# A fused test-time-training layer and mixture of experts: the low half of X1 taken ahead of the inverse's blocks, and the blocks spread by two rounded products

## The reference

```python
K, V, Q = x @ theta_K.T, x @ theta_V.T, x @ theta_Q.T
def step(W, b, k, v, q):
    g = 2 / 512 * (W @ k + b - v)
    W, b = W - 0.01 * outer(g, k), b - 0.01 * g
    return W, b, W @ q + b
x = layernorm(x + run_over_tokens(step))
shared = silu(x @ sW1 + sb1) @ sW2 + sb2
act = sqrt(softplus(x @ routing_W.T + expert_bias))
w, idx = top_k(act, 2)
x = layernorm(x + shared + sum_j w[j] * expert[idx[j]](x))
```

## Time and profile before

| | us |
|---|---|
| median of 3 runs (2300.41 to 2303.6) | 2301.88 |
| the profiled execution | 2296.03 |
| its span, first to last instruction | 2294.2 |
| PE busy | 2193.5 |
| DVE busy | 1548.6 |
| ACT busy | 891.7 |
| POOL busy | 1225.2 |
| mean granted clock of PE, 1 is full | 0.987 |

### The profile page before, as it was taken

One profiled execution on the slowest core, in us unless ns is written; L12 is line 12 of the kernel. 1 busy time (PEld: TensorE's weight loads), 2 busy tenths in 40 slices (PEclk: granted clock), 3 DMA queues, 4 the chain that ended last, 5 costly groups with the idle time before them and its releaser, 6 DMA issues.

```text
span 2294.2 us, 40089 instructions
## 1 busy us (share of the span) xinstructions
PE 2193.5 (96%) x12834; PEld 1899.8 (83%) x12834; DVE 1548.6 (68%) x3666; ACT 891.7 (39%) x1943; POOL 1225.2 (53%) x1168
## 2 busy tenths in 40 slices
PE   7999999999999999999999999999889999999896
PEld 6888888888888888888888888888779998998775
DVE  5666666666566778666656667775546545898798
ACT  4333333333333333333333334232255555555444
POOL 1344444433444333755544554346457777777777
PEclk9999999999999999999999999999989999999998
DMA  4211212122211111112211111110564435997996
GB/s 172 74 65 65 74 65 83 65 76 82 74 65 65 40 45 37 55 65 78 80 46 38 37 47 38 39 37 20 223 232 139 145 114 188 305 305 247 314 330 216
DMA packets 112201, 257.18 MB, mean 112 GB/s; under 512 B 21618, under 2 KB 23282, under 8 KB 109056
## 3 DMA queue, kind: packets, MB, share of 16 engines
q1 hardware_dynamic: 83776, 187.35, 23.5%
q0 software_dynamic: 27936, 67.22, 8.8%
q10 hardware_dynamic: 288, 0.04, 0.0%
HBM read 160.36 MB, written 105.26 MB: 116 GB/s over the span
## 4 chain that ended last, share of the span: by engine, by line
PE 77%; DVE 13%; issue 4%; POOL 2%; DMA 2%; ACT 1%; DVEq 0%; SPq 0%; POOLq 0%; ACTq 0%
PE banks L115 23%; PE banks L116 22%; PE banks L117 22%; PE banks L121 4%; DVE xc L1118 3%; PE banks L762 2%; PE banks L503 1%; PE banks L789 1%; DVE W L1115 1%; DVE b_Y L1118 1%; DVE banks L1115 1%; PE banks L541 1%; DVE X1l L1115 1%; DVE b_small L1661 1%; DMA W<-wd 1%
## 5 line engine op out<-in xcount | busy, mean ns | idle before, releaser
L115 PE MATMUL banks<-W 128*128 128x512 f32 (+1 forms) x2040 | 752.5, 369 | 10.8 <-DVE W L1115 7.6
L117 PE MATMUL banks<-W 128*128 128x512 f32 (+1 forms) x2040 | 718.0, 352 | 0.0
L116 PE MATMUL banks<-W 128*128 128x512 f32 (+1 forms) x2040 | 716.9, 351 | 0.0
L115 PEld LDWEIGHTS banks<-W 128*128 128x128 f32 x2040 | 387.9, 190 | 59.8 <-DVE W L1115 7.6
L117 PEld LDWEIGHTS banks<-W 128*128 128x128 f32 x2040 | 386.8, 190 | 54.8
L116 PEld LDWEIGHTS banks<-W 128*128 128x128 f32 x2040 | 388.3, 190 | 46.9
L1718 POOL TENSOR_TENSOR W<-S,W 128x512 fp32r<-128x512 f32 (+1 forms) x249 | 326.3, 1337 | 134.8 <-ACT W L833 134.2
L833 ACT ACTIVATE W<-banks 128x512 fp32r<-128x512 f32 x320 | 191.0, 598 | 503.3 <-DVE banks L1115 232.7
L1718 POOL TENSOR_TENSOR X<-X,B 128x1024 f32<-128x1024 f32 x32 | 76.8, 2401 | 459.0 <-DMA X<-in_x 459.0
L833 ACT ACTIVATE W<-S 128x512 fp32r<-128x512 f32 (+1 forms) x256 | 161.7, 653 | 219.5 <-DVE S L1115 213.2
L1115 DVE TENSOR_TENSOR W<-banks,W 128x512 fp32r<-128x512 f32 x192 | 132.4, 690 | 139.3 <-ACT W L833 139.2
(11 more groups left out here) (164 smaller groups left out, 4414.2 us busy)
## 6 DMA issues: line engine op xcount, KB each, us to landing
RG<-ys SPq DMA_DIRECT2D x128, 256.0 KB, 4.0
XT<-in_xT SPq DMA_DIRECT2D x32, 512.0 KB, 3.6
X<-in_x SPq DMA_DIRECT2D x32, 512.0 KB, 3.5
x1d<-X SPq DMA_DIRECT2D x64, 256.0 KB, 2.1
wd<-RG SPq DMA_DIRECT2D x32, 512.0 KB, 3.9
W<-wd SPq DMA_DIRECT2D x16, 1024.0 KB, 12.6
out<-b_Y SPq DMA_DIRECT2D x64, 256.0 KB, 4.4
zd<-X SPq DMA_DIRECT2D x52, 256.0 KB, 2.0
```

The lines of the kernel that those rows point to most:

```text
L115: e.matmul(o, ll, rh, start=start, stop=False, skip_group_check=True)
L116: e.matmul(o, lh, rl, start=False, stop=False, skip_group_check=True)
L117: return e.matmul(o, lh, rh, start=False, stop=stop, skip_group_check=True)
```

## The change

There are three edits.

1. In DVE's loop `turn_x1(t - 1, 1)`, which makes X1l of sequence 1, moves from behind `inv_m(t)` and the low half of P to a place ahead of `inv_m(t)`.
2. The compact form gd is written over the scores in their PSUM bank, where nothing else needs those columns once all three `rows_of` have read them; so these three now stand ahead of the sum. The unit products read it from there.
3. The compact form is split: gdh is its rounded part (scaled by -LRC), `rest` what is left of it, in PSUM too. The unit pattern multiplies each of them, four instructions instead of two, into two tiles in fp32r. `spread_blocks` is two products in fp32r with the block mask as the stationary operand, which is now an fp32r tile `blocks` of its own, made by a copy on ACT at the start. The two tiles take the memory of the inverse's halves (MTs, before MTh and MTl) and of the shared expert's hidden halves (Hp, before HH and HL), and waits keep the users apart: DVE's unit products wait for the last U and the last `down_x1`, ACT's `inv_end` and the writes of the hidden halves wait for the spread.

```diff
@@ memory
-        k.R = k.MM[:, 0:BLK]
-        k.xc, k.gd, k.rw = sb("xc", [NB, BS]), sb("gd", [NB, BS]), sb("rw", [KC, E])
+        k.Rp = k.MTs[:, 0:BLK], k.Hp[:, 0:BLK]
+        k.gdh = sb("gdh", [NB, BS], F32R)
+        k.xc, k.rw = sb("xc", [NB, BS]), sb("rw", [KC, E])
@@ tensor_program, spread_blocks
-        w.wait_ge(k.s_R, 2 * t + 2)
-        mm(e, o[:, 0:BLK], k.cst[:, 2, :], k.R).then_inc(k.s_Lb, 1)
+        w.wait_ge(k.s_R, 4 * t + 4)
+        mm(e, o[:, 0:BLK], k.blocks[:], k.Rp[1], True, False)
+        mm(e, o[:, 0:BLK], k.blocks[:], k.Rp[0], False, True).then_inc(k.s_Lb, 1)
@@ scalar_program
     def inv_end(t):
...
+        w.wait_ge(k.s_Lb, t + 1)
...
     def half_x1(t, b):
...
+        w.wait_ge(k.s_Lb, t + 2)
...
-    copy(k.onesr[:], k.RG[:, 0:P]).then_inc(k.s_ones, 1)
+    copy(k.onesr[:], k.RG[:, 0:P])
+    copy(k.blocks[:], k.RG[:, 2 * P:3 * P]).then_inc(k.s_ones, 1)
@@ vector_program, scores
-        rows_of(0).then_inc(k.s_sc, 1)
-        gd = k.gd[:]
-        w.wait_ge(k.s_sc, 4 * t + 2)
+        for n in range(NL):
+            z = rows_of(n)
+        z.then_inc(k.s_sc, 1)
+        gd = g[:, :, 0:BS]
+        w.wait_ge(k.s_sc, 6 * t + 2)
         e.tensor_reduce(gd, k.T1[:].rearrange("p b (k j) -> p b j k", k=NBL), AX.X, ALU.add).then_inc(k.s_sc, 1)
-        w.wait_ge(k.s_sc, 4 * t + 3)
-        w.wait_ge(k.s_MThi, t)
-        w.wait_ge(k.s_MTlo, t)
-        for h, o in enumerate(block_rows(k.R)):
-            rows = [P, HS, NB, (BS, HS)[h]]
-            own = unit_lr[:, h * HS:(h + 1) * HS].unsqueeze(2).unsqueeze(3)
-            tt(o, gd[:, :, h * HS:BS].unsqueeze(1).to_broadcast(rows), own.to_broadcast(rows), ALU.mult).then_inc(k.s_R, 1)
-        rows_of(1)
-        rows_of(2)
-        w.wait_ge(k.s_R, 2 * t + 2)
+        w.wait_ge(k.s_sc, 6 * t + 3)
+        e.tensor_scalar(k.gdh[:], gd, -LRC, None, ALU.mult).then_inc(k.s_sc, 1)
+        w.wait_ge(k.s_sc, 6 * t + 4)
+        rest = g[:, :, BS:2 * BS]
+        stt(rest, gd, -LRC, f32(k.gdh[:]), ALU.mult, ALU.subtract).then_inc(k.s_sc, 1)
+        w.wait_ge(k.s_sc, 6 * t + 5)
+        w.wait_ge(k.s_U, 2 * t)
+        w.wait_ge(k.s_dn1, min(2 * (t - 1), k.late))
+        for part, x, u in zip(k.Rp, (gd, rest), (unit_lr, unit)):
+            for h, o in enumerate(block_rows(part)):
+                rows = [P, HS, NB, (BS, HS)[h]]
+                own = u[:, h * HS:(h + 1) * HS].unsqueeze(2).unsqueeze(3)
+                tt(o, x[:, :, h * HS:BS].unsqueeze(1).to_broadcast(rows), own.to_broadcast(rows), ALU.mult).then_inc(k.s_R, 1)
+        w.wait_ge(k.s_R, 4 * t + 4)
@@ vector_program, the loop over t
+        if t > 0:
+            turn_x1(t - 1, 1)
         inv_m(t)
         next(first, None)
         if t > 0:
-            turn_x1(t - 1, 1)
             logits(t - 1, 0)
```

More of the change, by code:

```diff
@@ L30 @@
 NL = len(LEVELS)
-NCST = 3
 GROUPS = [14, 12, 6]
@@ L303, in first_memory @@
         k.X1p = sb("X1h", [KC, P], F32R), sb("X1l", [KC, P], F32R)
-        k.HF1, k.Hp1 = sb("HF1", [H]), (sb("HH1", [H], F32R), sb("HL1", [H], F32R))
+        k.HF1, k.Hp = sb("HF1", [H]), sb("Hp1", [2 * H], F32R)
+        k.Hp1 = k.Hp[:, 0:H], k.Hp[:, H:2 * H]
         k.brows, small = sb("brows", [D]), sb("small1", [40])
@@ L319, in first_memory @@
         k.ATp = sb("ATh", [NB, P], F32R), sb("ATl", [NB, P], F32R)
-        k.MTp = sb("MTh", [NB, P], F32R), sb("MTl", [NB, P], F32R)
-        k.onesr, k.cst = sb("onesr", [P], F32R), sb("cst", [NCST, P])
-        k.R = k.MM[:, 0:BLK]
-        k.xc, k.gd, k.rw = sb("xc", [NB, BS]), sb("gd", [NB, BS]), sb("rw", [KC, E])
+        k.MTs = sb("MTs", [2 * NB * P], F32R)
+        k.MTp = tuple(k.MTs[:, j * NB * P:(j + 1) * NB * P].rearrange("p (b n) -> p b n", b=NB) for j in range(2))
+        k.onesr, k.blocks, k.cst = sb("onesr", [P], F32R), sb("blocks", [P], F32R), sb("cst", [NB, P])
+        k.Rp = k.MTs[:, 0:BLK], k.Hp[:, 0:BLK]
+        k.gdh = sb("gdh", [NB, BS], F32R)
+        k.xc, k.rw = sb("xc", [NB, BS]), sb("rw", [KC, E])
 def second_memory(k):
@@ L545, in inv_t @@
         o = bank(w, ("T", t, n), k.s_T1, NL * t + n + 1)
-        w.wait_ge(k.s_sc, 4 * t + (4 if n else 2))
+        w.wait_ge(k.s_sc, 6 * t + 2)
         w.wait_ge(k.s_M0, NL * t + n + 1)
@@ L866, in scores @@
         kq = at["A", t].rearrange("p (b k n) -> p b k n", b=NB, k=2)[:, :, 1, :]
-        w.wait_ge(k.s_sc, 4 * t + 4)
+        w.wait_ge(k.s_sc, 6 * t + 6)
         w.wait_ge(k.s_O, 2 * t)
@@ L925, in half_x1 @@
         w.wait_ge(k.s_HS1, i + 1)
-        copy(k.Hp1[0][:], at["HB", t, b][:, 0:H]).then_inc(k.s_HH1, 1)
+        w.wait_ge(k.s_Lb, t + 2)
+        copy(k.Hp1[0], at["HB", t, b][:, 0:H]).then_inc(k.s_HH1, 1)
     def split_shared():
@@ L1100, in vector_program @@
     at = k.banks.at
-    mAT, mBD = k.cst[:, 0:2, :], k.cst[:, 2, :]
+    mAT, mBD = k.cst[:], f32(k.blocks[:])
     unit, unit_lr = k.smallc[:, 16:32], k.smallc[:, 136:152]
@@ L1141, in scores @@
         w.wait_ge(k.d_tab, 80)
+        w.wait_ge(k.s_ones, 1)
         w.wait_ge(k.s_T, NL * t)
@@ L1150, in scores @@
         stt(k.T1[:], g, 1.0, mBD.unsqueeze(1).to_broadcast(bc), ALU.add, ALU.mult).then_inc(k.s_sc, 1)
-        rows_of(0).then_inc(k.s_sc, 1)
-        gd = k.gd[:]
-        w.wait_ge(k.s_sc, 4 * t + 2)
-        e.tensor_reduce(gd, k.T1[:].rearrange("p b (k j) -> p b j k", k=NBL), AX.X, ALU.add).then_inc(k.s_sc, 1)
-        w.wait_ge(k.s_sc, 4 * t + 3)
-        w.wait_ge(k.s_MThi, t)
-        w.wait_ge(k.s_MTlo, t)
-        for h, o in enumerate(block_rows(k.R)):
-            rows = [P, HS, NB, (BS, HS)[h]]
-            own = unit_lr[:, h * HS:(h + 1) * HS].unsqueeze(2).unsqueeze(3)
-            tt(o, gd[:, :, h * HS:BS].unsqueeze(1).to_broadcast(rows), own.to_broadcast(rows), ALU.mult).then_inc(k.s_R, 1)
-        rows_of(1)
-        rows_of(2)
-        w.wait_ge(k.s_R, 2 * t + 2)
+        for n in range(NL):
+            z = rows_of(n)
+        z.then_inc(k.s_sc, 1)
+        gd = g[:, :, 0:BS]
+        w.wait_ge(k.s_sc, 6 * t + 2)
+        e.tensor_reduce(gd, k.T1[:].rearrange("p b (k j) -> p b j k", k=NBL), AX.X, ALU.add).then_inc(k.s_sc, 1)
+        w.wait_ge(k.s_sc, 6 * t + 3)
[12 more added lines that the diff above has]
+        w.wait_ge(k.s_R, 4 * t + 4)
         stt(kq, kq, -1.0, mAT, ALU.add, ALU.mult).then_inc(k.s_sc, 1)
         hi, lo = k.ATp
-        w.wait_ge(k.s_sc, 4 * t + 4)
+        w.wait_ge(k.s_sc, 6 * t + 6)
         w.wait_ge(k.s_AThi, t + 1)
@@ L1271, in back_x1 @@
         w.wait_ge(k.s_dn1, i)
-        tt(lo[:], at["HB", t, b][:, 0:H], f32(hi[:]), ALU.subtract).then_inc(k.s_HL1, 1)
+        w.wait_ge(k.s_Lb, t + 2)
+        tt(lo, at["HB", t, b][:, 0:H], f32(hi), ALU.subtract).then_inc(k.s_HL1, 1)
     def down_x1(t, b):
@@ L1977, in sync_program @@
     e.dma_start(k.idt[:], a["ids"]).then_inc(k.d_tab, 16)
-    e.dma_start(k.RG[:, 0:2 * P], a["ones"]).then_inc(k.d_lev, 16)
+    e.dma_start(k.RG[:, 0:3 * P], a["ones"]).then_inc(k.d_lev, 16)
     w.wait_ge(k.s_thlo, KC)
@@ L2116, in constants @@
     upto = (r <= c) * -1.0
-    masks = np.stack([upto[back][:, back], upto, np.repeat(blocks, BS, 1) * 1.0], 1), np.concatenate([np.ones((P, P)), up * 1.0], 1)
+    masks = np.stack([upto[back][:, back], upto], 1), np.concatenate([np.ones((P, P)), up * 1.0, np.repeat(blocks, BS, 1) * 1.0], 1)
     return [np.ascontiguousarray(x.astype(np.float32)) for x in (*masks, np.concatenate(levels, 1), blocks)]
```

## The result

| | before | changed |
|---|---|---|
| median of 4 runs each, side by side | 2302.74 (2300.41 to 2308.31) | 2268.02 (2267.31 to 2269.15) |
| ratio, 95% interval | | 0.9846 [0.9828, 0.9865] |
| the profiled execution | 2296.03 | 2267.31 |
| its span | 2294.2 | 2265.5 |
| mean granted clock of PE | 0.987 | 0.988 |

The kernel is 34.7 us faster by the medians, and 2268.0 us stands beside a forecast of 2269.5. The two profiled executions differ by less, 28.7 us of span: the one of before lay 6.7 us under its median, the one of the changed kernel 0.7 us under its own.

What follows compares the result with a forecast made beforehand. TensorE, busy 96%, was taken as the bound, with a recurring wait on X1l. Terms 13.9 + 2.7 + 1.3 + 2.5 + 2.7 + 9.3 = 32.4 us, off the median 2301.9, gave 2269.5 us; range 2260 to 2282.

Steps and rivals of the forecast that it cites:

- the whole 1.16 us: TensorE's idle gap before the first X1l product, steps 2 to 14: forecast to vanish entirely, 12 x 1.16 = 13.9 us.
- M0 as the next bound: Once X1l comes earlier, TensorE's product on ScalarE's copy M0 limits next; it had 0.55 us of slack.
- The product on it, due at 660.7, waits for nothing: Steps 2 to 14: M0 ends at 660.5, so TensorE's product on M0 at 660.7 has no wait.
- rival 1: M0 becomes the wait in every step: 12 steps lose 0.45 us each, 18 to 26 gain nothing; 2278 us, chance 0.22.
- M0's wait is above 0.3 us in steps 2 to 14: Sign that the prediction is wrong: TensorE waiting over 0.3 us on M0 in steps 2 to 14.
- none in 2 to 14: Expected sign: no TensorE wait on M0 in steps 2 to 14, about 0.5 us in steps 18 to 26.
- rival 4: VectorE's scores: products fed from PSUM stand still too, 0.5 us lost a step, 16 us slower, 2318 us; chance 0.03.
- the normalisations in steps 18 to 26 would get longer: VectorE's two normalisations of X, 2.24 us held behind GpSimd, were to lengthen, absorbing most of the products' extra 1.0 us.
- rival 3: TensorE's spread: the two rounded products are no faster than the old records, so it gains nothing; 2279 us, chance 0.03.
- the longer preparation doesn't show: VectorE's longer preparation of the spread costs nothing, since its products are ready 5.9 us before TensorE needs them.
- Steps 1 and 15 to 17: Gains forecast from gaps on X1l and the spread's 0.30 us a step: 0.6 us and 2.2 us.
- Rival 2: Later normalisations cost nothing: steps 18 to 26 keep 0.85 us, late steps all, clock stays up; 40 us, 2262, chance 0.15.

## Why the prediction was right, and where it was not

**The total.** Two errors cancelled. The sum of 32.4 us is 3.7 us more than the 28.7 us that the two profiled executions differ by. And I kept the 5.9 us that lay between before's profiled execution and its median; the changed kernel's profiled execution lay 0.7 us below its median. That is 5.2 us the other way, and no run shows why the two distances differ. That the median came out 1.5 us from the forecast is partly luck. The mechanism and most terms hold by themselves, as the stages show.

**Part 1, the gap on X1l.** On sequence 1, whose X1l was moved, it closed in every step of 2 to 26 (0.07 us was left in step 15); on sequence 0 the one wait, in step 15, grew from 0.36 to 0.71 us. The move alone gave 24.65 us where 23 were expected, some 2.5 of them by the clock. The term "the whole 1.16 us" was mis-sized, though, and so was its rival. Idle time in the trace is less than what a gap costs: a product that follows at once starts some 0.16 to 0.24 us before the end that is shown for the one ahead of it (the spread product at 634.75 ends at 635.09, the next one starts at 634.92). From the product starts in step 12 the gap cost 1.41 us. It works against me as well: ahead of the product on M0 TensorE shows 0.12 us idle in steps 2 to 13, and that costs 0.34 us, as the runs without that wait show (50.49 - 50.14 = 0.35). So 1.41 + 0.30 - 0.34 = 1.37 us a step, where I had 1.16 + 0.30 = 1.46.

**M0 as the next bound.** Named rightly and placed almost rightly. Put on the old time axis by the spread (649.44 - 634.58 = 14.86 us), GpSimd's additions ended at 657.0 as forecast, the block matrix at 657.3 (forecast 657.2), the subtraction started at 657.9 (657.8), and M0 ended at 660.6 (660.5). "The product on it, due at 660.7, waits for nothing" is the step that failed: it was due 0.28 us before its 660.75, since the gap ahead of it was worth more. (With M0's copy moved it starts 12.06 us behind the first product of dB, in the changed kernel 12.34.) So the wait that rival 1 names came in all of steps 2 to 14, at 0.34 us and not 0.45. Of my signs of being wrong, "M0's wait is above 0.3 us in steps 2 to 14" is not met by the idle time shown and is met by what the wait costs; "none in 2 to 14" is missed by both. In steps 18 to 26 I gave 0.55 us for the wait. 0.48 to 0.58 us of idle time is shown, and the cost is 0.70 us a step (50.90 - 50.20). That these steps still gain 0.65 us, beside a forecast of 0.6, is two errors again: X1l's gap there, 0.83 to 0.88 us shown, was worth more as well, about 1.1 us by the same 0.25 us.

**Part 2, PSUM.** The new products take 280 to 425 ns, as from the rows of T, and never stand still; rival 4 (slower) is out, and the kernel with the compact form in SBUF is what its mechanism looks like, though by the rest and not by the four products. The two small ones took 0.19 and 0.20 us. One sentence was wrong by my own argument: I wrote that the normalisations in steps 18 to 26 would get longer. They come later into the same wait and got shorter, 1.38 us for the pair in step 20 against 2.24.

**Part 3, the spread.** 0.30 us a step was forecast. Measured: two products 0.17 us apart and the next one 0.30 us earlier, so rival 3 is out, and 0.32 us a step between the two kernels with M0 moved. But "the longer preparation doesn't show" was wrong. It doesn't delay the spread, which is ready long before. It does delay GpSimd's additions (in step 12 they end 8.60 us behind the first product of dB, and 7.87 with the preparation unsplit), and so the block matrix and M0: with the preparation unsplit the block matrix takes 416 ns, and no wait ahead of MM,LT is shown in steps 2 to 14 and 18 to 26. I looked for those who wait for R and not for what stands behind it in VectorE's queue.

**Steps 1 and 15 to 17.** Forecast 0.6 and 2.2 us, measured -0.15 and 0.4, or 2.1 in the two executions at the full clock. In step 1 the block matrix had fallen between two GpSimd instructions before (0.42 us) and met one now (1.02 us). In step 15 the wait ahead of MM,LT grew from 0.8 to 1.8 us, and the step gained 0.1 us only; steps 16 and 17 made up for it. I had taken these from the sum of X1l's gaps, not from what stands behind them, so the agreement at 2.1 us is in part luck.

**Steps 27 to 31.** 3.2 of 4.0 us, some 0.9 of it by the clock. The earlier trace rows less leave 6.9 us of gaps behind 1400 us where I counted 3.7; the 3.0 us of step 31 are in them, and stayed.

**Rival 2.** It had steps 18 to 26 keep the whole gap and the clock stay up more. They gained 6.1 us, where it needed over 10, and up to step 30 both executions have two stretches of 3.4 us at half the clock: they moved, and none went away.
